# Causal attention: stacks three groups ahead issued ahead of the fold of the totals, and the last part of queries and keys one side later on GpSimd

## The reference

```
q = q * cos + rotate_half(q) * sin        # layer 0 only, k likewise
scores = einsum('bqhd,bkhd->bhqk', q, k) / sqrt(8)
scores = where(causal, scores, -1e30)
p = softmax(scores); y = einsum('bhqk,bkhd->bqhd', p, v)
```

## Time and profile before

| | us |
|---|---|
| median of 3 runs | 5636.39 (5633.79 to 5652.36) |
| the profiled execution | 5639.38 |
| its span | 5637.6 |
| TensorE, VectorE, ScalarE, GpSimd busy | 4852.8, 3790.4, 3198.8, 1906.2 |
| mean granted clock of TensorE | 0.946 |

### The profile page before, as it was taken

One profiled execution on the slowest core, in us unless ns is written; L12 is line 12 of the kernel. 1 busy time (PEld: TensorE's weight loads), 2 busy tenths in 40 slices (PEclk: granted clock), 3 DMA queues, 4 the chain that ended last, 5 costly groups with the idle time before them and its releaser, 6 DMA issues. The chain is left out here.

```text
span 5637.6 us, 167378 instructions
## 1 busy us (share of the span) xinstructions
PE 4852.8 (86%) x74160; PEld 2833.7 (50%) x74352; DVE 3790.4 (67%) x4626; ACT 3198.8 (57%) x3838; POOL 1906.2 (34%) x1342
## 2 busy tenths in 40 slices
PE   7868887996888599988998899979998799889997
PEld 4523333443333266645665466636664466536663
DVE  5657772334777488847886588748884688658884
ACT  4536663222666477735775477636774577546773
POOL 1320000003000155505553355515551455325560
PEclk9979998997999899999999999989999999999998
DMA  0011110002111111101111011101111111101111
GB/s 24 11 63 39 35 35 30 0 0 64 34 34 40 45 37 39 36 32 36 37 40 44 22 39 36 36 32 37 39 36 35 32 36 40 47 18 39 36 40 39
DMA packets 96672, 196.92 MB, mean 35 GB/s; under 512 B 27312, under 2 KB 45872, under 8 KB 93872
## 3 DMA queue, kind: packets, MB, share of 16 engines
q1 hardware_dynamic: 95920, 185.86, 12.8%
HBM read 64.13 MB, written 15.73 MB: 14 GB/s over the span
## 5 line engine op out<-in xcount | busy, mean ns | idle before, releaser
L1499 POOL TENSOR_TENSOR part_of_local<-part_of_local,sine_of_local 128x512 f32<-128x512 f32 x768 | 960.2, 1272 | 1062.2 <-DVE sine_of_local L1436 1062.2
L897 ACT ACTIVATE prob_of_ca<-ps 128x1024 f32<-128x1024 f32 (+3 forms) x768 | 596.6, 813 | 332.1 <-PE ps L771 231.6
L1506 POOL TENSOR_TENSOR part_of_local<-part_of_local,inverse_of_local 128x1024 f32<-128x1024 f32 x384 | 722.1, 1902 | 144.1 <-DVE inverse_of_local L1468 144.1
L1473 DVE TENSOR_REDUCE total_of_local<-prob_of_local 128x16 f32<-128x1024 f32 x192 | 234.3, 1220 | 415.7 <-ACT prob_of_local L1412 415.7
L1433 DVE TENSOR_TENSOR part_of_local<-ps,rope 128x1024 f32<-128x1024 f32 x384 | 466.7, 1215 | 46.4 <-ACT square_of_local L1380 46.4
L789 PE MATMUL ps<-keys_of_ca,queries_of_ca 64*128 64x512 bf16 (+3 forms) x1536 | 335.1, 346 | 184.0 <-DVE top_of_ca L929 68.8
L1272 PE MATMUL ps<-qkv,shifted 128*128 128x512 f32 x768 | 396.3, 639 | 84.9 <-POOL values_of_local L1509 79.7
L1436 DVE TENSOR_TENSOR sine_of_local<-ps,rope 128x1024 f32<-128x1024 f32 x384 | 466.5, 1215 | 0.0
L1282 PE MATMUL ps<-qkv,shifted 128*128 128x512 f32 x768 | 383.2, 622 | 73.7 <-ACT heads_out_of_local L1408 60.0
L1358 PEld LDWEIGHTS ps<-prob_t_of_local,mixed_of_local 64*64 64x64 f32 x12288 | 341.0, 134 | 161.3 <-issue 150.3
L1367 PE MATMUL ps<-heads_out_of_local,wo 128*128 128x128 f32 x3072 | 392.3, 283 | 14.4 <-ACT heads_out_of_local L1408 14.0
(11 more groups left out here) (198 smaller groups left out, 9798.5 us busy)
## 6 DMA issues: line engine op xcount, KB each, us to landing
mixed_of_local<-values_of_local SPq DMA_DIRECT2D x636, 128.0 KB
mixed_of_local<-values_of_local SPq DMA_DIRECT2D x264, 64.0 KB
queries_of_ca<-q_parts SPq DMA_DIRECT2D x384, 32.0 KB
keys_of_ca<-k_parts SPq DMA_DIRECT2D x384, 32.0 KB
qkv<-in_qkv SPq DMA_DIRECT2D x7, 1536.0 KB, 6.3
rope<-in_rope SPq DMA_DIRECT2D x7, 1024.0 KB, 8.8
q_parts<-parts_of_ci SPq DMA_DIRECT2D x16, 384.0 KB, 2.5
k_parts<-parts_of_ci SPq DMA_DIRECT2D x16, 384.0 KB, 2.5
```

The costliest lines, as they stand in the source:

```text
L897: nc.scalar.activation(prob[:, i % 2, 2 * two:2 * two + 2, j:], ps[:, 2 * two:2 * two + 2, j:], ACT.Exp, scale=scale).then_inc(raised, 1)
L1499: nc.gpsimd.tensor_tensor(out, out, sine[:, side, :, (1 - to) * half:(2 - to) * half], ALU.add).then_inc(rotated, 1)
L1506: nc.gpsimd.tensor_tensor(part[:, t % 2, side], part[:, t % 2, side], by, ALU.mult).then_inc(scaled, 1)
```

## The change

Two orders are changed, and no instruction is added or removed. On GpSimd the low part goes two sides behind the addition instead of one. On SyncE the load of the stack three groups on stands behind the collection and ahead of the fold; it waits for the same scores and goes into the same slot as before. Group 0 and the last groups get the same loads as before.

```diff
-                for i in range(SIDES + 1):
+                for i in range(SIDES + 2):
                     if rotated and i < SIDES:
                         add(i)
-                    if i:
-                        leave_low(i - 1)
+                    if i >= 2:
+                        leave_low(i - 2)
...
                 for G in range(ALL):
-                    if G and G + 2 < ALL:
-                        sp.wait_ge(scored, 2 * NU * G)
-                        load_stack(sp, loaded[(G + 2) % RING_CA], stacks, zeros, q_parts, k_parts, G + 2)
                     if G + 1 < ALL:
                         place(G + 1)
                     collect(G)
+                    if G + RING_CA < ALL:
+                        sp.wait_ge(scored, 2 * NU * (G + 1))
+                        load_stack(sp, loaded[G % RING_CA], stacks, zeros, q_parts, k_parts, G + RING_CA)
                     if G % GROUPS == GROUPS - 1:
                         fold(G // GROUPS)
```

## The result

| | before | after |
|---|---|---|
| median | 5635.31 us (20 runs) | 5650.08 us (20 runs) |
| the profiled execution's span | 5637.6 us | 5651.0 us |

The changed kernel is slower: the ratio of the runs is 1.0026, with a 95% interval of 1.0018 to 1.0035. On 5635 us that is +14.8 us by the medians and 10 to 20 us by the interval. The forecast was +20.5, for a time of 5657 us within 5643 to 5672.

The account below looks back on a forecast made before the run. It took SyncE's queue behind six folds (48.8 us over ordinary groups) and the inputs' closed ring as bounds. Loads +53 - 24.6 + 1.5 = +30, inputs -9.5, total +20.5 on 5636.4: 5657 us, range 5643 to 5672.

Parts of the forecast that it names:

- VectorE's wait at unit 5: At the inversion behind a fold, VectorE stands 9.2 us for the folded totals instead of 0.53, with TensorE held behind it.
- The delay of the fold: At six folds, SyncE fetches the totals 8.7 us later, behind the load; the path gets 6 x 8.8 = 53 us.
- The waits at unit 8: TensorE's six waits for the stack's last transfer, in groups behind a fold, go: -24.6 us.
- The low clock: TensorE's 1.2 GHz stretches behind stalls in the six groups: today's 15.8 us cost stays, plus 1.5 us in all.
- rival A: Loads +50, waits -24.6, low clock 3 us cheaper as it lies partly in idle time, inputs -12: +10, 5647 us; chance 0.24.
- Together +30: Sum for SyncE's loads ahead of the fold: +53 - 24.6 + 1.5 = +30 us.
- GpSimd's order: First layer's inputs: the low part one side later gives 2.96 us a side; -(14.8 - 4.1 - 1.2) = -9.5 us.
- SyncE's stack behind side 5 and the stall it makes: First layer's inputs: ScalarE's stall at side 10 grows from 1.0 to 6.6 us; net -4.1 us of the gain.
- The 1.2 us for TensorE's low level: First layer's inputs: TensorE's slack goes and its 1.2 GHz level takes 1.2 us off the gain.
- B: Fetch of folded totals queues behind the load's packets and the low clock lasts: +20.5 + 15, 5672 us; chance 0.08.
- C: SyncE issues the 26 transfers in under 1.3 us, so the fold is not delayed: -50, 5586 us; chance 0.05.
- D: First layer's inputs: the ring is closed elsewhere, for example at the store's landing, so GpSimd's edit gives 0: 5667 us; chance 0.10.

Follow-up runs that it names:

- half_ahead: Changed kernel with 12 of the stack's 26 issues ahead of the fold and 14 behind it, at the six places; 5611.0 us in one execution.
- late_alone: Kernel before, both old orders kept, with only VectorE's reciprocal moved from unit 5 to unit 8; 5680.4 us in one execution.
- best: Changed kernel with the reciprocal at unit 8 and the first stack's 26 issues spread behind nine stores of the inputs; 5558.7 us against 5633.0, ratio 0.9884.
- only_low: Kernel before with only GpSimd's low part one side later, SyncE's order as before; 5623.2 us, ratio 0.9993.

## Why the prediction was right, point by point

The direction, the place and the mechanism held: slower, by VectorE's wait at unit 5. The size of the total is in part luck, as the sum below shows. Of the terms:

**The delay of the fold, forecast +53 us.** The reciprocal starts 16.00, 16.45, 16.14, 16.48, 16.03 and 16.03 us after the collection, together 97.1 against 45.8 before: +51.3 us. At the first fold the reciprocal is 8.30 us later and TensorE's wait 8.31 us longer (10.00 against 1.69), so all of it reaches the path. The forecast was 0.25 us a fold too high: four of the six loads took 9.6 us, and it had counted 9.95 for all.

**The waits at unit 8, forecast -24.6 us.** They are gone.

**The low clock, forecast +1.5 us.** This term was mis-sized. Of the six groups' 239.9 us, 171.3 are six ordinary groups, 8.4 the inversions and 51.3 the delay. That leaves 8.9 us for the clock where it was 15.8: -6.9 us. I had weighed a gain (rival A) and kept the cost as it was because the idle stretch is longer. The granted clock around the first stall of the changed kernel (stretch, length, the engines' busy times, PEclk, DMA share, GB/s):

```profile
506.00:510.00 4.00, 3.95 (x62) 1.68 (x54) 3.36 (x6) 2.38 (x5) 0.00 (x0) 1.00 0.23 49
511.50:514.50 3.00, 0.00 (x0) 0.00 (x0) 0.00 (x0) 1.32 (x2) 0.00 (x0) 1.00 0.35 94
515.00:521.00 6.00, 0.00 (x0) 0.00 (x0) 1.55 (x2) 0.00 (x0) 0.00 (x0) 0.50 0.16 47
521.30:524.80 3.50, 3.50 (x20) 0.82 (x22) 1.73 (x2) 0.26 (x1) 0.00 (x0) 0.51 0.48 121
526.00:530.00 4.00, 2.89 (x25) 0.62 (x24) 3.22 (x4) 2.46 (x3) 2.49 (x2) 1.00 0.01 3
```

and around that of the kernel before:

```profile
531.50:535.00 3.50, 0.00 (x0) 0.00 (x0) 0.39 (x2) 0.66 (x1) 0.00 (x0) 1.00 0.31 84
535.50:536.30 0.80, 0.00 (x0) 0.00 (x0) 0.00 (x0) 0.00 (x0) 0.00 (x0) 0.50 0.04 10
536.40:541.70 5.30, 5.30 (x41) 2.21 (x41) 1.38 (x2) 1.84 (x2) 0.00 (x0) 0.50 0.00 0
543.00:545.00 2.00, 2.00 (x31) 0.81 (x29) 1.52 (x2) 0.81 (x1) 0.00 (x0) 1.00 0.01 4
```

In the changed kernel TensorE is idle from 511.3 to 521.27. The clock is still 1.00 in the first 3 us of that and at 0.50 for 6 us in which nobody uses it, and then 3.5 us of work run at the low level, 1.2 GHz, until 524.8. In the kernel before, the clock fell 4.3 us into an idle stretch of 5.3, and 5.3 us of work ran low behind it. Over the six stalls the work at the low level is 28.0 us before (2.9 to 8.6 each) and 20.5 after (3.1 to 3.8 each). If half of that is loss, which is an estimate, the gain is 3.7 us; the other 3 of the 6.9 are a remainder that no row explains.

Why less work ran low is not shown. Rival A's argument, that a longer stall hides more of its own low clock, is borne out at unit 5: stalls of about 4.6 us in `half_ahead` leave 4.8 us of low work each, stalls of 10 us in the changed kernel 3.4. It is not borne out at unit 8: stalls of 3.0 to 5.3 us in the kernel before leave 4.7 us each, stalls of 15 us in `late_alone` 5.7. The figures that the prediction gave for the fall (about 3 us) and for the low work (3 to 9 us) are near the 2.3 to 4.3 and 2.9 to 8.6 us of that trace.

**Together +30, measured +19.8 us**: -1.7 by the delay, -8.4 by the clock. With the inputs the forecast's +20.5 us becomes +11.3 by the traces, close to rival A's +10. The medians say +14.8, and the 3.5 us between are not placed in any term. That the time came out clearly slower rests on them as well.

**GpSimd's order, forecast -9.5 us, measured -8.5.** The ring opened as described. A side takes 3.08 us (two stores in 309.82 - 303.66 = 6.16) instead of the 2.96 worked out: 15 x 0.87 = 13.1 us of gain for 14.8, of which 4.6 came back, for 5.3. In the timeline above VectorE's subtraction comes second at 303.77 and takes 1.64 instead of 0.69 us, through to the end of GpSimd's addition; then GpSimd's subtraction comes second at 304.82 and is stretched to 1.60. So the block goes both ways. It is full but for a constant end: the overlaps are 1.09, 0.59 and 0.58 us (the last in the earlier trace rows), the stretches 0.95, 0.45 and 0.45, each 0.13 or 0.14 us less. I had taken a partial block of GpSimd alone from one row. By the rule of the Trainium skill that I set beside it (SBUF — State Buffer, "Who interferes with whom") the one that comes second is fully blocked, and a side would be 3.1 us. The trace agrees with the page, with 3.08, and not with my 0.78, though the sum is another: GpSimd loses 0.45 us a side by the stretch and 0.28 by waiting for VectorE. SyncE's stack behind side 5 and the stall it makes, forecast 6.6 us at side 10:

```profile
312.62 0.36 SPq L574 DMA_DIRECT2D k_parts<-parts_of_ci  x1
...
323.98 0.40 SPq L574 DMA_DIRECT2D q_parts<-parts_of_ci  x1
...
326.66 0.63 ACT L530 ACTIVATE parts_of_ci<-value_of_ci 128x512 bf16<-128x512 f32 x1 [8.26 <-DMA q_parts<-parts_of_ci]
```

ScalarE's idle time there is 8.26 us, and at the other even sides it is 2.65, so the stall is 5.6 us (the expectation of `best` counts the whole 8.3). The store of side 6 is issued 11.4 us after that of side 5, close to the 11.3 of before, and lands as fast. The 1.2 us for TensorE's low level are not there: its clock is at 0.50 from 326.8 to 333.6 us, and the sides behind follow each other as those ahead of it do. The term of this stage is right within 1 us.

**Rivals.** B (fetch queued behind the load's packets) is out: the reciprocal starts 1.80 us after the fetch's issue (519.45 - 517.65), where it was 1.89 without a load ahead of it (521.40 - 519.51). C would have needed 26 issues in under 1.3 us; they take 9.5. D is out with `only_low`'s stage. A was right in that the low clock costs less than before, and the result (+14.8) lies between it (+10) and the forecast (+20.5). Both stand at the ends of the interval of 10 to 20 us, so the time alone does not tell which is nearer.

Of the six lengths in the prediction the third is 35.65 us in the trace, not 35.68; their sum of 48.8 us over the ordinary length is right.

## What to carry to other kernels

A transfer that is issued too late on an in-order queue can be cured by moving it ahead of its neighbour only if the neighbour's own deadline is checked too. Here a load of 9.6 us of issue time was put ahead of a fetch that was already 0.5 us late, with a consumer in the middle of the critical order. Look for the place where the consumer of the delayed result has idle time of its own (here, three units on, VectorE stands behind a copy anyway); moving both ends together gained 1% where each alone lost.

## What the runs showed of the hardware that was not expected

- VectorE's elementwise operation on two SBUF tiles (128x512 fp32) and GpSimd's operations on SBUF tiles block each other, whichever starts second: VectorE's took 1.64 us instead of 0.69, GpSimd's 1.71 instead of 1.26 and 1.60 instead of 1.15. The stretch was the overlap less 0.13 or 0.14 us each time. With one of VectorE's inputs in PSUM neither was stretched (0.69, 1.27 and 1.17 us).
- In the kernel before, TensorE's clock fell 2.3 to 4.3 us after the engine had gone idle; at the stalls of 3.05 and 2.98 us it fell 1.2 us after work had begun again, so that even these were followed by 2.9 and 3.1 us of work at 1.2 GHz. Behind stalls of 10 us 3.1 to 3.8 us of work ran low, behind stalls of 15 us 3.6 to 11.7.
- The load of a stack takes 9.6 us of SyncE's issue time while its last transfer landed 2.0 us after its issue, and the DMA engines were busy 0.35 of the time from 511.50 to 514.50 us: for these transfers the issuing queue is the bound, not the DMA engines.
